# The state scan and the attention layers in one block, and B's rows loaded from DRAM instead of multiplied out

## The reference, cut to what matters

```python
def step(s, inp):                       # 16 states n for each of 256 inner channels
    d, u_i, b_i, c_i = inp
    s = s * jnp.exp(d[..., None] * A) + (d * u_i)[..., None] * b_i[:, None, :]
    y = jnp.einsum('bdn,bn->bd', s, c_i)
    return (s, y)
...
y = y + u * D_skip; y = y * silu(z); x1 = y @ out_proj_w.T       # then x1 + x0, rms norm, MLP with relu, residual
...
# attention, per layer: token shift, qkv, l2 norm, rotary, windows of 64 keys (own and last), softmax, @ wo
# then token shift, layer norm, h @ w1, a * gelu(g), @ w2
```

## Time and profile before

| | us |
|---|---|
| median of 3 runs | 1678.2 |
| the profiled execution, whole | 1673.4 |
| its span in the trace | 1671.6 |
| scan, first to last state on DVE | 461.3 to 918.7 |
| chain of the last chunk, then the barrier | 925.4 to 953.6 |
| attention | 953.6 to 1671.6 |
| busy PE, DVE, ACT, POOL over the span | 1368.5, 1240.6, 1086.1, 927.7 |

### The profile page before, as it was taken

How to read it: one execution, slowest core, us unless ns; L and a number is a source line. 1 busy time by engine, 2 the same in 40 slices (tenths; PEclk the granted TensorE clock), 3 DMA queues, 4 the chain that set the end, 5 groups by cost and what they waited for, 6 DMA issues and landing times. The chain is left out here.

```text
span 1671.6 us, 23460 instructions
## 1 busy us (share of the span) xinstructions
PE 1368.5 (82%) x8131; PEld 734.8 (44%) x8150; DVE 1240.6 (74%) x1782; ACT 1086.1 (65%) x1847; POOL 927.7 (55%) x484
## 2 busy tenths in 40 slices
PE   6748068667767888888888668999999999999987
PEld 2216067522223333333333335555555555555553
DVE  2974145338689989999989189888888888888863
ACT  4423045278856666666666258888888888888874
POOL 0440624300598888788888057555555556666641
PEclk9867589888789999999999789999999999999999
DMA  1005421210000000003000011111111111121110
GB/s 65 1 0 95 132 58 53 75 48 0 3 1 0 1 1 1 0 1 133 0 1 0 15 39 32 46 27 45 27 45 27 45 27 46 33 52 33 39 26 26
DMA packets 49001, 54.21 MB, mean 32 GB/s; under 512 B 10434, under 2 KB 32116, under 8 KB 48500
## 3 DMA queue, kind: packets, MB, share of 16 engines
q1 hardware_dynamic: 46580, 47.98, 11.6%
q0 software_dynamic: 2304, 4.74, 0.9%
HBM read 20.15 MB, written 9.47 MB: 18 GB/s over the span
## 5 line engine op out<-in xcount | busy, mean ns | idle before, releaser
L1153 POOL TENSOR_TENSOR ssm_dbu<-ssm_dtu,ssm_b_all 128x1024 f32<-128x1024 f32 x128 | 299.5, 2362 | 43.6 <-ACT ssm_b_all L1077 43.4
L1782 POOL TENSOR_TENSOR at_direct<-at_direct,home_dt 128x1024 f32<-128x1024 f32 x64 | 152.3, 2380 | 287.1 <-DVE home_dt L1872 287.1
L940 PE MATMUL ssm_bank<-ssm_seen,ident 128*128 128x512 f32 x512 | 249.6, 611 | 40.0 <-POOL ssm_seen L1162 37.8
L1071 ACT ACTIVATE ssm_bank<-home_dt,ssm_decay 128x512 f32<-128x512 f32 x256 | 173.2, 691 | 60.7 <-DVE ssm_state L1255 59.3
L1255 DVE TENSOR_TENSOR_SCAN ssm_state<-ssm_bank,ssm_dbu 128x512 f32<-128x512 f32 x128 | 149.0, 1208 | 20.1 <-POOL ssm_dbu L1153 13.3
L1255 DVE TENSOR_TENSOR_SCAN ssm_state<-ssm_bank,ssm_carry,ssm_dbu 128x512 f32<-128x512 f32 x128 | 156.3, 1266 | 7.3 <-ACT ssm_bank L1071 4.6
L940 PEld LDWEIGHTS ssm_bank<-ssm_seen,ident 128*128 128x128 f32 x512 | 96.8, 194 | 126.5 <-issue 67.2
L1077 ACT ACTIVATE ssm_b_all<-ssm_bank 128x512 f32<-128x512 f32 x128 | 75.8, 592 | 103.1 <-PE ssm_bank L917 79.6
L1565 PE MATMUL at_two<-home_u,at_hs 128*128 128x512 f32 x256 | 129.2, 628 | 9.6 <-ACT at_kT L1712 5.6
L1787 POOL TENSOR_TENSOR home_u<-home_u,at_inv 128x1024 f32<-128x1024 f32 x64 | 121.5, 1898 | 18.6 <-DVE at_inv L1883 18.6
L1793 POOL TENSOR_TENSOR at_direct<-at_direct,at_rnorm 128x1024 f32<-128x1024 f32 x64 | 123.1, 1924 | 0.2
(11 more groups left out here) (237 smaller groups left out, 3318.0 us busy)
## 6 DMA issues: line engine op xcount, KB each, us to landing
at_v_mix<-at_v SPq DMA_DIRECT2D x112, 128.0 KB, 2.4
at_hs<-branch SPq DMA_DIRECT2D x64, 128.0 KB, 2.3
moe_w<-in_moe_w SPq DMA_DIRECT2D x16, 256.0 KB
moe_to_experts<-moe_empty SPq DMA_DIRECT2D x10, 258.0 KB, 7.9
moe_slot_rows<-moe_to_experts SPq DMA_DIRECT2D x10, 258.0 KB, 2.9
x<-in_x SPq DMA_DIRECT2D x8, 256.0 KB, 3.5
moe_rows<-moe_from_experts SPq DMA_DIRECT2D x8, 256.0 KB, 4.8
home_dt<-in_turn SPq DMA_DIRECT2D x2, 1024.0 KB
```

The costliest lines, as they stand in the source:

```text
L940: last = nc.tensor.matmul(bank[Y0 + half][:], ident[:], seen[:, n % 2, half], start=False, stop=n == STATES - 1)
L1071: nc.scalar.activation(bank[DA0 + half][:], chunk_of(dt[:, half], t), ACT.Exp, scale=decay[:, half, n:n + 1]).then_inc(r[f"da{half}"], 1)
L1153: nc.gpsimd.tensor_tensor(dbu[:, i % RING], dtu[:, t % 2], b_all[:, i % 2:i % 2 + 1, :].broadcast_to([P, 2, CH]), ALU.mult).then_inc(r["db ...
L1782: nc.gpsimd.tensor_tensor(direct[:, n % TURNED], direct[:, n % TURNED], crossed[:, n % 2], ALU.add).then_inc(s["added"], 1)
```

## The change

It does three things.

1. **B's rows.** Ahead of the scan ACT copies the 16 rows of B of each chunk as float32 (`b_low`), and SP stores them to a DRAM buffer `b_rows` (16 x 4096). In the scan, SP loads for each step the 2 KB of `b_rows[n]` onto all 128 partitions of `b_all`, now a ring of 4: one DMA that writes 256 KB a step, 128 in all. The load of step i is issued when `dbu` of step i - 4 is done. PE's product for B and ACT's copy of it are gone, in all 128 steps. `pick` is half as large. The loads of the attention's operands, issued in one go before, are now issued one by one between B's loads, in steps 92 to 125.
2. **One block.** The attention is no block of its own with a barrier ahead of it. Each of its steps is called from the scan's loop at i = 128, 131, 134, ... (with a lag of 4 steps on PE and ACT, of 2 on POOL and DVE) behind the posted work of that step, so seven attention steps of DVE and six of PE and ACT stand between the links of the last chunk's chain. What remains of the attention follows the loop. DVE begins with `vector_start` at i = 130, PE with `tensor_start` at i = 132; `tables(1)` and `fold()` are moved from g = 2 to g = 0. The SBUF of the scan's rings is reused, hence waits for the last y (`r["y"]`) and for the last chunk's chain.
3. **Layout.** Some attention buffers are placed elsewhere in the reused memory (qk, square, prob, pT, oT, hidden), and the PSUM banks of the scan are renumbered so that both stages fit together.

```diff
@@ sync, in the stage of the scan
+            for t in range(2 * SEQS):
+                sp.wait_ge(s["b_low"], done(t))
+                sp.dma_start(b_rows[:, t * CH:(t + 1) * CH], rest[0:STATES, t % 2]).then_inc(b_stored[t % 2], 16)
...
+            for i in range(ALL_STEPS):
+                t, n = divmod(i, STATES)
+                if real(i - B_RING):
+                    sp.wait_ge(r["dbu"], up_to(i - B_RING))
+                    sp.wait_ge(b_loaded[i % B_RING], 16 * (i // B_RING))
+                sp.dma_start(b_all[:, i % B_RING], b_rows[n:n + 1, t * CH:(t + 1) * CH].partition_broadcast(P)
+                             ).then_inc(b_loaded[i % B_RING], 16)
+                if i == FROM:
+                    sp.wait_ge(r["ready"], SEQS)
+                if FROM <= i < FROM + len(loads):
+                    to, of = loads[i - FROM]
+                    sp.dma_start(to, of).then_inc(r["operands"], 16)
...
+            attend.sync_program()
@@ tensor
-                if real(i):
-                    t, n = divmod(i, STATES)
-                    if real(i - 1):
-                        pe.wait_ge(r["b_all"], up_to(i - 1))
-                    nc.tensor.matmul(bank[B0][:], pick[:, n], chunk_of(parts, t), start=True, stop=True
-                                     ).then_inc(r["b"], 1)
...
+                if i == OPENS + BEHIND:
+                    attend.tensor_start()
+                if attended(i - BEHIND) is not None:
+                    attend.tensor_step(attended(i - BEHIND))
+            for g in range(attended_through(LAST_STEP - BEHIND), LAST + 1):
+                attend.tensor_step(g)
@@ scalar
+                    act.wait_ge(b_stored[k], b * 16 + 16)
+                    nc.scalar.activation(rest[0:STATES, k], bank[k][0:STATES, :], ACT.Copy).then_inc(s["b_low"], 1)
...
-                if real(i):
-                    act.wait_ge(r["b"], up_to(i))
-                    if real(i - 2):
-                        act.wait_ge(r["dbu"], up_to(i - 2))
-                    nc.scalar.activation(b_all[:, i % 2], bank[B0][:], ACT.Copy).then_inc(r["b_all"], 1)
...
+                if attended(i - BEHIND) is not None:
+                    attend.scalar_step(attended(i - BEHIND))
@@ gpsimd
-                    pool.wait_ge(r["b_all"], up_to(i))
+                    pool.wait_ge(b_loaded[i % B_RING], 16 * (i // B_RING + 1))
@@ vector
+                if i == OPENS + AHEAD:
+                    attend.vector_start()
+                if attended(i - AHEAD) is not None:
+                    attend.vector_step(attended(i - AHEAD))
...
+    def vector_start():
+        dve.wait_ge(r["y"], up_to(ALL_STEPS - 1))
+        dve.wait_ge(r["operands"], OPERANDS)
+        nc.vector.memset(hs[64:128, :, 0:1], 0.0).then_inc(s["edge"], 1)
+        nc.vector.memset(hs2[64:128, :, 0:1], 0.0).then_inc(s["edge"], 1)
+        tables(0)
...
+        if g == 0:
+            tables(1)
+            fold()
...
-STAGES = [min_gru, experts, mamba, ffn]
+STAGES = [min_gru, experts, mamba_and_attention]
```

More of the change, by code:

```diff
@@ L9 @@
+from collections import namedtuple
 from contextlib import ExitStack
@@ L748 @@
 SSM = ("folded zeroed decay decay_ready uz raw tap z conv0 conv1 "
-       "conv u dbc dt_low hi rest1 mid rest2 parts dtraw size small over dtlog dt")
-SCAN = ("dtu b c b_all c_all da0 da1 dbu state0 state1 carried seen seen_apart y gated out branch "
+       "conv u dbc dt_low b_low hi rest1 mid rest2 parts dtraw size small over dtlog dt")
+SCAN = ("dtu c c_all da0 da1 dbu state0 state1 carried seen seen_apart y gated out branch "
         "weights fc3 fc1_folded squared power logged rstd normed joined up hidden0 half hidden1 down x "
@@ new lines, in attention @@
+    total = sb("total", [P, 2, HEADS])
+    inv = sb("inv", [P, 2, HEADS])
+    power = sb("power", [P, CH])
+    ln = sb("ln", [P, CH])
+    rstd = sb("rstd", [P, CH])
+    two = ctx.enter_context(nc.psum_tensor("at_two", [P, 2, CH], F32))
+    scores = ctx.enter_context(nc.psum_tensor("at_scores", [P, 2, CH], F32))
+    one = ctx.enter_context(nc.psum_tensor("at_one", [P, CH], F32))
+    glu = [ctx.enter_context(nc.psum_tensor(f"glu_bank{n}", [P, CH], F32)) for n in range(3)]
+    GATE_BANK, VALUE_BANK, WO_BANK, VARIANCE_BANK, DOWN_BANK = (1, 2, 0), (2, 0, 2), 1, 2, 0
@@ new lines, in tensor_start @@
+    def tensor_start():
+        pe.wait_ge(r["operands"], OPERANDS)
+        for layer in range(LAYERS):
+            for m in range(2):
+                for p, (first, size) in enumerate(HID_PARTS):
+                    at = (layer * 2 + m) * PARTS_OF_HID + p
+                    last = nc.tensor.matmul(glu[0][0:size, at:at + 1],
+                                            w1[:, layer, m * HID + first:m * HID + first + size],
+                                            ln_b[:, layer:layer + 1], start=True, stop=True)
+        last.then_inc(s["lb_done"], 1)
@@ new lines, in root, with gelus @@
+    def root(c):
+        act.wait_ge(s["variance"], up_to(c))
+        nc.scalar.activation(ln[:], glu[VARIANCE_BANK][:], ACT.Ln, bias=EPS_LN).then_inc(s["logged"], 1)
+        act.wait_ge(s["logged"], up_to(c))
+        if c >= 1:
+            act.wait_ge(s["normed"], up_to(c - 1))
+        nc.scalar.activation(rstd[:], ln[:], ACT.Exp, scale=-0.5).then_inc(s["rooted"], 1)
+    def gelus(c):
+        if c >= 1:
+            act.wait_ge(s["down"], up_to(c - 1))
+        for p, (first, size) in enumerate(HID_PARTS):
+            act.wait_ge(s["gates"], c * PARTS_OF_HID + p + 1)
+            nc.scalar.activation(hidden[p][0:size], glu[GATE_BANK[p]][0:size, :], ACT.Gelu,
+                                 bias=b1[0:size, c // LAYER_CHUNKS, 1, p:p + 1]).then_inc(s["gelu"], 1)
@@ new lines, in vector_start, with tables @@
+    def vector_start():
[4 more added lines that the diff above has]
+        tables(0)
+    def tables(layer):
+        for n in range(2):
+            nc.vector.tensor_tensor(turn[layer][:, n], turn[layer][:, n],
+                                    scales[:, layer, n].unsqueeze(1).broadcast_to([P, TILES, 2, HEAD]),
+                                    ALU.mult).then_inc(s["tables"], 1)
@@ new lines, in fold @@
+    def fold():
+        dve.wait_ge(s["lb_done"], 1)
+        for layer in range(LAYERS):
+            for p, (first, size) in enumerate(HID_PARTS):
+                at = glu[0][0:size, layer * 2 * PARTS_OF_HID:(layer + 1) * 2 * PARTS_OF_HID]
+                nc.vector.tensor_tensor(b1[0:size, layer, :, p], b1[0:size, layer, :, p],
+                                        at.rearrange("p (m c) -> p m c", m=2)[:, :, p], ALU.add)
+        for layer in range(LAYERS):
+            last = nc.vector.tensor_scalar(w1[:, layer], w1[:, layer], ln_g[:, layer:layer + 1], None,
+                                           ALU.mult)
+        last.then_inc(s["folded"], 1)
```

1062 lines of the change are left out of this document (524 added, 538 removed).

## The result

The changed kernel takes **1651.2 us** (median of four runs, 1647.2 to 1653.9) against 1678.6 for the kernel before on the same chip: ratio 0.9838, 95% interval 0.9814 to 0.9863. The forecast was 1653, range 1636 to 1674. The total is right to 2 us; its two large terms are not.

A forecast was written before the change was run, and what follows sets the result against it. DVE, 94% busy, was taken to bound the scan and PE the attention from about its sixth tile. Gains of 15 (scan) and 12 (merge) less 2 ahead of the scan make 25 us: 1678.2 to 1653 us, range 1636 to 1674.

The forecast's parts named there:

- Part 1, the scan: Scan: taking B's copies from ACT and POOL's waits for them gains 15 us, bounds 5 and 24.
- I allow 1 us of waiting for each of 8 chunks: Scan: allowance for DVE's waiting when POOL has dt*u and the residual addition besides, once a chunk.
- the 11.0 us should nearly go: Scan: DVE's 11.0 us in 23 waits for ACT's decay nearly vanish without the copies of B.
- that leaves 11 of the 26.1 us: Scan: of DVE's 26.1 us idle, 11 us remain, which gains 15 us.
- level: at most 3 us in 32 places: Scan: POOL's next dbu comes about when DVE asks, at most some 0.1 us of waiting in each of 32 places.
- Part 1, the loads: Scan: B's row loads land in 3.5 us, are hidden by 3 us and cost 0; far bound 5 us.
- Rival B: Scan: row loads set the pace and the kernel turns slower, 1752 us at a 14 us landing; chance 0.08.
- Part 1, ahead of the scan: Ahead of the scan: eight added copies of B on ACT lose 2 us, bounds 0 and 5.
- Part 2: Last chunk's chain merged with the attention's start: earlier attention gains 12 us, bounds 5 and 20.
- The fold and tables: Attention start: `tables(1)`, moved ahead of POOL's first step, takes 2.36 us instead of 4.49.
- Rival A: Merge: chain links and attention steps add up without overlap, so it gives 0; 1672 us, chance 0.09.
- C: Scan: TensorE's clock falls because PE has less to do, costing 44 us; 1697 us, chance 0.03.

The follow-up runs named there:

- without the burst: Changed kernel with POOL's dt*u split into halves ahead of states 4 and 8 and the residual addition moved to state 12; 1635.8 us, ratio 0.9753.
- the ring of two: Changed kernel with POOL's dt*u halved and residual addition at state 12, plus two buffered rows of B instead of four; ratio 0.9785.
- rows multiplied out: Changed kernel, but B's rows are again multiplied out on PE and copied by ACT, without row loads or B's copies and stores ahead; 1655.4 us, ratio 0.9869.
- every fifth step: Changed kernel with POOL's dt*u halved and residual addition at state 12, plus attention steps five scan steps apart instead of three; ratio 0.9836.

## Why the prediction was right, and its terms were not

- **What bounds the kernel:** right. DVE's busy time stayed (431.3 to 430.3 us) and PE binds the attention; the gain at the sixth tile, 80.6 - 55.5 = 25.1 us, is still 25.7 at the last qk copy. In the last 80 us 3.8 of it were lost, at a granted clock of 0.77 from 1584 to 1599 us and 0.92 at the end, where before had 1.00 in the last 47. Two windows of after, in the columns above:

```profile
1584.00:1599.00 15.00, 11.41 (x91) 6.38 (x90) 4.56 (x6) 6.92 (x9) 3.54 (x2) 0.77 0.08 19
...
1629.00:1649.30 20.30, 13.88 (x27) 4.70 (x26) 5.09 (x7) 5.85 (x7) 0.00 (x0) 0.92 0.07 26
```

- **Part 1, the scan, -15 forecast, -3.7 measured, outside my bound of 5:** the term that failed. Three of its steps did. "I allow 1 us of waiting for each of 8 chunks" for POOL's dt*u and addition: this is worth 16.7 us, taken away by spreading them, which is 2.1 us a chunk, or 2.8 in each of the six chunks that have both. And "the 11.0 us should nearly go": the decay's waits fell to 5.8, but of the 5.2 us won 2.9 came back as waits for dbu at the same steps. I had read the releasers' sums as if each were a separate cost. They were one lateness with several names, and the copies of B hardly lay on its path: without the burst they cost 1.9 us. Third, "that leaves 11 of the 26.1 us" also counts the 6.8 us ahead of seen as gone, and the prediction gives no reason for that; 6.2 us (3.8 and 2.4) stayed, and they too went with the burst. One step, "level: at most 3 us in 32 places", holds: 1.1 us are left once the burst is gone.
- **Part 1, the loads:** right. 3.1 us to landing against 3.5 assumed, no wait for a DMA, the operand loads between the rows harmless with a ring of four. Rival B was far off; the ring of two puts a price near the edge, 3.7 us. The Trainium skill, page DMA: Bandwidth & Descriptors, section Issuing engines are not separate DMA queues, warned of interleaving; at 84 GB/s over the scan no run with the ring of four shows a cost of it. The prediction's 2.6 us, an estimate from the Trainium skill's page DMA: Bandwidth & Descriptors, section Anatomy of one DMA — SWDGE (gpsimd) path, was 0.5 too low; the fit there is for DMAs issued by GpSimd, and these are issued by SP.
- **Part 1, ahead of the scan:** +2 forecast, +1.6 measured; over the runs, without and with the copies, 96.5 and 96.7 to 98.4 in the first round, 97.3 and 99.3 to 99.8 in the second, 97.1 and 96.8 to 98.5 in the third: 1 to 2 us.
- **Part 2, -12 forecast, -21.9 measured, outside my bound of 20:** the mechanism is right, the size too small. By marks:

| counted from Y, us | before | forecast, full and half clock | after | rows multiplied out |
|---|---|---|---|---|
| first qk copy starts | 37.1 | 11.7 | 8.4 | 8.8 |
| last chunk's output added | 3.6 | 12 | 8.0 | |
| first MLP layer on PE | | 25 | 19.5 | 21.3 |
| second MLP layer on PE | | 32 | 25.5 | 28.5 |
| first scores shifted | 63.7 | 43.5, 51.4 | 37.7 | 40.7 |
| sixth tile's sums start | 80.6 | 63.6, 72.3 | 55.5 | 58.4 |

  Three pieces. The start: the small products took 2.45 us, not 4.69, and the first qk copy and the fold came 3 to 4 us sooner. PE's granted clock was 1.00 (the level of 2.4 GHz) in those products; before it was 0.50, behind 3.33 us of idle PE. The lines are before, then after:

```profile
953.70:958.40 4.70, 4.69 (x24) 4.60 (x24) 2.48 (x4) 1.24 (x1) 0.00 (x0) 0.50 0.56 134
...
928.40:930.90 2.50, 2.50 (x26) 2.47 (x25) 2.50 (x3) 0.00 (x0) 0.00 (x0) 1.00 0.64 151
```

  The links to the second MLP layer: another 3 us; I had stacked the chain's steps on the attention's where they ran beside each other; that is read from the marks and no run tests it alone. And the clock: I priced half clock as 9 us and took the middle. With the rows multiplied out the clock behind Y was as low as in any run (0.76 over 28 us), yet the mark comes only 2.9 us later than after, as the clock is at 1.00 from the 28th microsecond on. Even there the gain at the mark is 22.2 us, so both ends of my 8 to 17 were too low.
- **The fold and tables:** right. Four products for the tables took 4.63 us together, 1.16 each, as fast as the pair before beside an idle POOL, and POOL is idle here too; the two scalings of w1 took 1.05 instead of 2.30 us. The Trainium skill, page SBUF — State Buffer, section Who interferes with whom, says that DVE and GpSimd share a pair of ports; the trace agrees.
- **The sum** came out by luck: 11.3 us too much in the scan met 9.9 too little in the merge. Rival A is excluded by the 25 us at the mark, C by a clock of 0.95 in the scan, against 0.97 before.

## What to carry to other kernels

Before costing the removal of work, look at the fullest engine's stalls one by one and in time: when they recur at the same steps of each round, ask which engine runs without a gap just ahead of them, for the sums by releaser spread one lateness over several names, and relieving an engine that is not on its path gives little (3.7 us here of 15 forecast). Extra work that comes once a round should be spread over the round, never two pieces at one place; here moving one addition by four steps gave 15.6 us in the scan, four times what the new data path gave. And where a serial chain and the start of the next stage are each latency bound, alternating them by hand gains most of the shorter one.

## What the runs showed of the hardware

- One DRAM row of 2 KB read onto all 128 partitions (256 KB written) lands in 3.1 us, 128 times in a row at 84 GB/s, and DVE's scans kept 1.20 us beside it, POOL's dbu 2.36.
- 24 products of one column each took 4.69 us at a granted clock of 0.50 (1.2 GHz), after 3.3 us of idle PE, and 2.45 us at 1.00 (2.4 GHz) right behind other products. The 2.45 us stand in every kernel with the single block, the 4.69 in both kernels with a barrier. Their ratio, 1.9, is close to that of the clocks.
- SP stood 6.71 us on one issue of a 1 MB load with 34 in a row, and 0.43 us on the same load when the issues came every 2 to 4 us.
- With every fifth step, the four runs follow the mean granted clock: 1637.2 us at 0.933, 1644.6 and 1645.2 at 0.929, 1648.9 at 0.925. The changed kernel's four don't: 1647.2 us at 0.926, 1651.2 at 0.927, with 1651.1 at 0.924 and 1653.9 at 0.925.
